# A six-product graph kernel: the first product sums x unprojected, with layer 1 behind the sum; the last half by blocks

## The chip, the cores and the metric

One core of a Trainium2 chip runs the whole kernel in one launch. The metric is the time on the device in microseconds, the median of several runs. Three runs of the kernel before took 1157.63, 1157.7 and 1158.45 us. Engines are called PE (TensorE), ACT (ScalarE), DVE (VectorE), POOL (GpSimd) and SP (SyncE, which issues most DMAs).

## What is computed

x is 4096 x 128, adj 4096 x 4096, every weight 128 x 128. Cut to what matters:

```python
def mlp(x, W1, b1, W2, b2, W3, b3):         # a = leaky_relu, slope 0.01
    return a(a(a(x @ W1 + b1) @ W2 + b2) @ W3 + b3)
u = x
for _ in range(3):
    v = mlp(adj @ u, uv_W1, uv_b1, uv_W2, uv_b2, uv_W3, uv_b3)
    u = mlp(adj @ v, vu_W1, vu_b1, vu_W2, vu_b2, vu_W3, vu_b3)   # the third u isn't needed
y = layernorm(x + v)
out = layernorm(y + adj @ (y @ gcn_W))
```

So adj is applied six times in a row (products 0 to 5), each time to something that depends on the product before.

## The kernel before

**Tiling.** A chunk is 512 nodes; there are 8. The sums are kept turned: features on the partitions, 512 nodes of the output chunk as columns, one PSUM bank each. adj is read in tiles of 128 x 1024 floats (2 x 128 input nodes times 512 output nodes). Two tiles are a band, 1 MB, one DMA. A visit multiplies one tile into one sum. Precision comes from splitting: ACT rounds a tile to `high` (L571), DVE makes `low` = raw - high (L728), and the same is done with the operand p (`p_high`, `p_low`). A visit is six products of 512 columns (L960): p_low x high and p_high x high for both halves of the tile, then p_high x low for both. Only the last two need `low`.

**Layer 1 before the sum.** Since adj @ (u @ W1) = (adj @ u) @ W1, each MLP's first layer is applied ahead of its product: `turn` multiplies a finished chunk by the next W1 and brings it back to nodes on the partitions; `raise_turned` and `lower_turned` split it into p. For product 0 this is `project_x` (PE, L893): x arrives turned, with uv_W1 in front of it (`x_turned`), is projected in FP32 chunk by chunk into PSUM banks, and ACT and DVE split it from there (`raise_x`, L575; `lower_x`, L733). x in the other order (`x_nodes`) is needed for the first layernorm's residual and is loaded into the same memory later (`load_residual`, at tile 200).

**A finished chunk.** ACT makes the first leaky layer out of the sum (`first_layer`, L623 rounded and L624 exact), DVE its low half (`lower_first`, L754), PE layer 2 in three products (`dense`, L866, L867, L869), and so on to layer 3 and the turn (`turning`, L900).

**Order of work.** `Plan` writes out by hand which visit comes when. All engines run through the same count n of visits, each in its own program order. What a chunk needs is placed at `chunk.start` plus an offset (`LOWER_FIRST`, `LAYER_2`, ... , `TURN`). ACT raises tile t `AHEAD` = 6 visits before its first visit (4 for tiles 16 to 31), DVE lowers it two visits later. SP loads bands in order; up to band 7 the loads wait for nothing, band 8 waits until DVE has lowered the tiles of band 4, band 9 for those of band 5 (a ring of four buffers). The first sweep does product 0 chunk by chunk, 16 tiles each; row c also takes the tiles of the columns 0 to c-1 a second time for product 1. `X_SPLIT` says ahead of which tile each chunk of x is split. `WARMING` FP32 products of zeros keep PE busy at first (L975).

**The tail.** The last chunk of product 5 is cut into two halves of 256 columns. Its first tiles are summed into a bank and kept in `part` (`keep`, L589). The last four tiles are visited for half 0 and then for half 1, each in a bank of its own. Per half, DVE adds bank and part (`finish_half`, L749), PE multiplies by gcn_W (`project`), DVE adds x (L787), takes statistics per block of 128 (L791, L794), ACT takes the root (L656), DVE the reciprocal (L802), and for half 1 DVE normalizes both blocks (`normalize_half`, L811).

Of the kernel before, what the change touches and what calls it, by code (L numbers as in the profile page):

```python
# [37 lines left out]
X_PIECES = [2, 2, 4]  # L38

X_SPLIT = [0, 0, 0, 0, 2, 4, 6, 8]  # L40

CONSTS_AT, OTHER_CONSTS_AT, RESIDUAL_AT = 12, 22, 200

WARMING = 9
# [11 lines left out]
FIRST = "uv_W1"  # L56
WEIGHTS = ["uv_W2", "uv_W3"]
OTHER_WEIGHTS = ["vu_W1", "vu_W2", "vu_W3", "gcn_W"]
SPLIT = ["uv_W2", "uv_W3", "vu_W2", "vu_W3"]
# [8 lines left out]

LOWER_FIRST, LAYER_2, LOWER_SECOND, LAYER_3 = 1, 3, 4, 6
# [8 lines left out]
HALF_PROJECT, HALF_MEASURE, HALF_ROOT, HALF_INVERT, HALF_NORMALIZE = 2, 3, 4, 5, 6  # L78
# [9 lines left out]
class Sum:  # L88

# [17 lines left out]
    seeded: int = -1  # L107

# [19 lines left out]
class Plan:  # L128
# [100 lines left out]
    def last_sweep(self):  # L229
# [9 lines left out]
        self.one(rows[-1], columns[:-IN_HALVES], self.open(LAST, rows[-1], "keep"))  # L239
        last = [self.tile(rows[-1], column) for column in columns[-IN_HALVES:]]  # L240
        for half in range(2):
            total = self.open(LAST, rows[-1], "finish")
            self.sums[total].half = half
            for t in last:
                self.visit(t, total)

    def place_chunks(self):
# [6 lines left out]
        for i in sorted(finished, key=lambda i: self.sums[i].closes):  # L254
            s = self.sums[i]
            if self.chunks:
                apart = SPACING[s.product] if s.product == self.sums[self.chunks[-1].total].product else BETWEEN
                s.read = max(s.read, self.chunks[-1].start + apart)
            s.finished = len(self.chunks)
            self.chunks.append(Chunk(i, s.read, s.read + (TURN if s.product < NORMED else NORM_TURN), s.half))  # L260
# [15 lines left out]
    def place_banks(self):  # L276

        holder = [None] * BANKS
        for i in sorted(range(len(self.sums)), key=lambda i: self.sums[i].opens):
            s = self.sums[i]  # L280
            s.bank = min(range(BANKS), key=lambda b: -1 if holder[b] is None else self.sums[holder[b]].read)
            if holder[s.bank] is not None:
# [19 lines left out]
def gnn_kernel(nc, adj, x_turned, x_nodes, constants, out):  # L302
# [4 lines left out]
    with ExitStack() as ctx:  # L307
# [17 lines left out]
        consts = sbuf("consts", [D, CONSTS])  # L325
        w = {name: consts[:, bass.ds(i * D, D)] for i, name in enumerate(WEIGHTS)}
        b_spread = consts[:, bass.ds(SPREAD_AT, D)]
        b = {name: consts[:, BIASES_AT + i:BIASES_AT + i + 1] for i, name in enumerate(BIASES)}
        w_high = {name: sbuf(f"w_high_{name}", [D, D], F32R) for name in SPLIT}
        w_low = {name: sbuf(f"w_low_{name}", [D, D], F32R) for name in SPLIT}  # L330

# [14 lines left out]
        sbuf("pad", [D, D])  # L346


        input_and_weight = sbuf("input", [D, D + N])
        w.update({name: consts[:, bass.ds(OTHERS_AT + i * D, D)] for i, name in enumerate(OTHER_WEIGHTS)})  # L350
        w[FIRST] = input_and_weight[:, 0:D]
        resid = input_and_weight[:, D:D + N]
# [12 lines left out]
        residual_loaded = sem("residual_loaded")  # L365
        consts_set = sem("consts_set")
        nothing_set = sem("nothing_set")
        table_loaded = sem("table_loaded")
        band_loaded = [sem(f"band_loaded{i}") for i in range(EARLY + RAWS // IN_BAND + LATE)]
# [9 lines left out]
        x_projected = sem("x_projected")  # L379
# [20 lines left out]
        normed_ready = sem("normed_ready")  # L400
        last_normed = sem("last_normed")
# [50 lines left out]
        def x_bank(c):  # L452

            return [proj, *layer, *acc[1:]][c % (BANKS + 2)]

# [11 lines left out]
        def blocks_in(i):  # L467
            half = chunks[i].half
            return range(IN_CHUNK) if half < 0 else range(half * IN_CHUNK // 2, (half + 1) * IN_CHUNK // 2)

# [43 lines left out]
        def _(sp):  # L514
            def load_x(piece):
                columns = slice(D + sum(X_PIECES[:piece]) * CHUNK if piece else 0, D + sum(X_PIECES[:piece + 1]) * CHUNK)
                sp.dma_start(input_and_weight[:, columns], x_turned[:, columns]).then_inc(x_loaded[piece], 16)

            def load_residual():
                sp.wait_ge(x_projected, CHUNKS)  # L520
                sp.dma_start(resid, x_nodes).then_inc(residual_loaded, 16)

            def load(t):
# [6 lines left out]
                sp.dma_start(band_in(buffer), adj[tiles[t][0], tiles[t][1] // IN_BAND]).then_inc(band_loaded[buffer], 16)  # L530

            for piece in range(len(X_PIECES)):
                load_x(piece)
            for t in range(0, len(tiles), IN_BAND):
                if t == CONSTS_AT:
                    sp.dma_start(consts[:, 0:OTHERS_AT], constants[:, 0:OTHERS_AT]).then_inc(consts_loaded, 16)
                if t == OTHER_CONSTS_AT:
                    sp.dma_start(consts[:, OTHERS_AT:CONSTS], constants[:, OTHERS_AT:CONSTS]).then_inc(others_loaded, 16)
                if t == RESIDUAL_AT:
                    load_residual()  # L540
                load(t)

            for i in (len(chunks) - 2, len(chunks) - 1):
                if chunks[i].half < 1:
                    sp.wait_ge(normed_ready, i - NORM + 1)
                else:
                    sp.wait_ge(last_normed, 1)
# [17 lines left out]
        def _(act):  # L565
            def split(t):
                buffer = buffers[t // IN_BAND]
                act.wait_ge(band_loaded[buffer], 16 * (len(loads_into(buffer, t // IN_BAND)) + 1))
# [4 lines left out]
            def raise_x(c):  # L573
                act.wait_ge(x_projected, c + 1)
                nc.scalar.activation(p_high[0][:, blocks_of(c)], x_bank(c)[:],  # L575
# [7 lines left out]
            def keep(s):  # L583
# [5 lines left out]
                nc.scalar.activation(part_of(s.chunk), acc[s.bank][:], ACT.Copy).then_inc(part_kept, 1)  # L589

            def seed(s):
# [5 lines left out]
                if before.goal == "keep":  # L597
                    act.wait_ge(part_kept, before.nth + 1)
                elif before.product < LAST:
# [17 lines left out]

            def first_layer(i):

                act.wait_ge(visited, sum_of(i).closes + 1)  # L620
                wait_free(i)
                bias = b[f"{way_of(i)}_b1"]
                nc.scalar.activation(h_high[:], summed(i)[:], ACT.Prelu, bias=bias, alpha=SLOPE).then_inc(first_raised, 1)  # L623
                nc.scalar.activation(h[i % 2][:], summed(i)[:], ACT.Prelu, bias=bias, alpha=SLOPE).then_inc(first_ready, 1)  # L624
# [33 lines left out]
            def normalize(i):  # L658
                act.wait_ge(shift_ready, i - NORM + 1)
                c = sum_of(i).chunk  # L660
                for j in blocks_in(i):
                    target = block_in(resid[:, blocks_of(c)] if normed(i) else part_of(c), j)
                    done = nc.scalar.activation(target, block_in(h[i % 2], j), ACT.Identity,
                                                bias=shift[:, j:j + 1], scale=rstd[:, j:j + 1])
                done.then_inc(normed_ready, 1)

# [10 lines left out]
            for n in range(END):  # L677
                if n == UV_HALVED:
                    raise_weights(SPLIT[:2])
                if n == VU_HALVED:  # L680
                    raise_weights(SPLIT[2:])
                for i, chunk in enumerate(chunks):
                    if layered(i):
                        if n == chunk.start:
# [16 lines left out]
                    if not layered(i):  # L701
                        if n == chunk.start and chunk.half < 0:
                            gather(i)
                        if n == place(i, LAST_ROOT, HALF_ROOT):
                            deviation(i)
                        if n == place(i, LAST_NORMALIZE, HALF_NORMALIZE) and chunk.half < 1:
                            normalize(i)
# [15 lines left out]
        def _(dve):  # L723
            nc.vector.memset(h[0][:, 0:D], 0.0).then_inc(nothing_set, 1)

# [5 lines left out]
            def lower_x(c):  # L731
                dve.wait_ge(p_high_ready, c + 1)
                nc.vector.tensor_tensor(p_low[0][:, blocks_of(c)], x_bank(c)[:],  # L733
# [8 lines left out]
            def finish_half(i):  # L742
# [6 lines left out]
                nc.vector.tensor_tensor(h[i % 2][:, columns], acc[s.bank][:, columns], part_of(s.chunk)[:, columns],  # L749
                                        ALU.add).then_inc(half_ready, 1)  # L750
# [18 lines left out]
            def add_bias(i):  # L769
                dve.wait_ge(proj_done, i + 1)  # L770
                nc.vector.tensor_tensor(
# [3 lines left out]
            def measure(i):  # L775

                if layered(i):
                    dve.wait_ge(leaky_done, i - NORM + 1)
                    dve.wait_ge(residual_loaded, 16)
# [6 lines left out]
                columns = columns_in(chunks[i].half)  # L786
                nc.vector.tensor_tensor(h[i % 2][:, columns], source[:, columns],  # L787
                                        resid[:, blocks_of(sum_of(i).chunk)][:, columns], ALU.add).then_inc(x_added, 1)
                dve.wait_ge(x_added, i - NORM + 1)
                for j in blocks_in(i):  # L790
                    nc.vector.bn_stats(stats[:, j, :], block_in(h[i % 2], j)).then_inc(stats_ready, 1)  # L791
# [16 lines left out]
            def normalize_half(i):  # L808

                for j in blocks_in(i):  # L810
                    done = nc.vector.tensor_scalar(block_in(part_of(sum_of(i).chunk), j), block_in(h[i % 2], j),  # L811
                                                   moments[:, j, 0:1], rstd[:, j:j + 1], op0=ALU.subtract, op1=ALU.mult)
                done.then_inc(last_normed, 1)
# [8 lines left out]
            for n in range(END):  # L822
                if n == UV_HALVED:
                    lower_weights(SPLIT[:2])
                if n == VU_HALVED:
                    lower_weights(SPLIT[2:])
                for i, chunk in enumerate(chunks):
                    if n == chunk.start and chunk.half >= 0:
                        finish_half(i)
                    if layered(i) and n == chunk.start + LOWER_FIRST:  # L830
# [15 lines left out]
                    if not layered(i):  # L846
                        if n == place(i, LAST_MEASURE, HALF_MEASURE):
                            measure(i)
                        if n == place(i, LAST_INVERT, HALF_INVERT):
                            invert(i)  # L850
                            if chunk.half == 1:
                                normalize_half(i)
# [9 lines left out]
        def _(pe):  # L862
# [7 lines left out]

            def layer_2(i):
                name = f"{way_of(i)}_W2"
                pe.wait_ge(w_low_ready, 2 if sum_of(i).product == 0 else len(SPLIT))
                if i:
                    pe.wait_ge(second_ready, i)
                else:
                    pe.wait_ge(p_low_ready, CHUNKS)
# [8 lines left out]
            def project_x(c):  # L886

                pe.wait_ge(x_loaded[0], 16)
                pe.wait_ge(x_loaded[piece_of(c)], 16)
                if c >= BANKS + 2:  # L890
# [136 lines left out]
```

## Time and profile before

| | |
|---|---|
| median of 3 runs | 1157.7 us |
| the profiled execution's own time | 1157.88 us |
| its span, first to last instruction | 1155.9 us |
| PE busy | 1149.8 us |
| DVE busy | 721.2 us |
| ACT busy | 726.6 us |
| DMA moved | 281.42 MB, mean 243 GB/s |

Busy time is summed per engine; matmuls overlap in the array, so the step from one start to the next tells more about PE than the duration of a record. A 128x128 FP32 product appears as two records. The chain is the row of work that ended last, followed back from the end: what is on it can't be shortened without the end moving, up to the point where something else is late. Idle time is given with what ended it.

### The profile page before, as it was taken

To read this page: it belongs to the slowest core of one execution; us is meant where nothing else is said; L and a number is where in the kernel's file an instruction comes from. 1 tells how busy PE (TensorE), PEld (TensorE's weight loads), DVE (VectorE), ACT (ScalarE), POOL (GpSimd) and SP (SyncE) were. 2 spreads that over 40 slices of the span, in tenths; PEclk is the share of its full clock that TensorE was granted. 3 is DMA by queue.
4 is the path that set the end of the run, shared out by engine and by line. 5 is a ranking of instruction groups with operands and counts; after the bars stand their busy time and mean duration, and the time that the engine had idled before them with its cause. 6 is when DMAs were issued, how large, how long until landed. Compare 5 with 4: busy or idle time off the path is not lost.

```text
span 1155.9 us, 14073 instructions
## 1 busy us (share of the span) xinstructions
PE 1149.8 (99%) x5314; PEld 961.3 (83%) x5314; DVE 721.2 (62%) x837; ACT 726.6 (63%) x925; POOL 4.2 (0%) x12
## 2 busy tenths in 40 slices
PE   9999999999999999999999999999999999999998
PEld 8888888888888888888888888888888888888887
DVE  6987545554665344765553585545558775459996
ACT  6876654455776444876554486544567874459884
POOL 0000000000000000000000000000000000000000
PEclk9999999999999999999999999999999999999999
DMA  9997656645855576666553584656558565579990
GB/s 384 387 365 274 231 197 244 229 178 195 319 185 207 190 276 234 242 231 255 218 182 145 196 349 182 224 197 234 198 196 327 206 230 191 216 274 371 373 382 22
DMA packets 39361, 281.42 MB, mean 243 GB/s; under 512 B 4416, under 2 KB 4800, under 8 KB 5632
## 3 DMA queue, kind: packets, MB, share of 16 engines
q1 hardware_dynamic: 38736, 278.69, 64.1%
q0 software_dynamic: 560, 1.84, 0.4%
q8 instruction: 44, 0.72, 0.2%
q14 instruction: 21, 0.17, 0.0%
HBM read 278.41 MB, written 2.10 MB: 243 GB/s over the span
## 4 chain that ended last, share of the span: by engine, by line
PE 99%; DVE 0%; issue 0%; ACT 0%; DVEq 0%
PE acc L960 90%; PE proj L900 4%; PE layer L869 1%; PE layer L866 1%; PE layer L867 1%; PE proj L975 0%; PE acc L893 0%; PE proj L893 0%; PE layer L893 0%; DVE stats L791 0%; DVE h L787 0%; DVE h L749 0%; DVE part L811 0%; ACT std L656 0%; DVEq L307 0%
## 5 line engine op out<-in xcount | busy, mean ns | idle before, releaser
L960 PE MATMUL acc<-high,p_low 128*128 128x512 f32 x1544 | 603.0, 391 | 0.0
L960 PE MATMUL acc<-high,p_high 128*128 128x512 f32 x1544 | 598.9, 388 | 0.0
L728 DVE TENSOR_TENSOR low<-raw,high 128x1024 fp32r<-128x1024 f32 x482 | 562.2, 1218 | 47.5 <-ACT high L571 46.8
L571 ACT ACTIVATE high<-raw 128x1024 fp32r<-128x1024 f32 x482 | 485.9, 1054 | 70.9 <-PE acc L960 49.0
L960 PE MATMUL acc<-low,p_high 128*128 128x512 f32 x1544 | 473.8, 388 | 0.0
L960 PEld LDWEIGHTS acc<-low,p_high 128*128 128x128 f32 x1544 | 289.1, 188 | 60.1 <-DVE low L728 0.5
L960 PEld LDWEIGHTS acc<-high,p_high 128*128 128x128 f32 x1544 | 290.1, 188 | 58.1
L960 PEld LDWEIGHTS acc<-high,p_low 128*128 128x128 f32 x1544 | 290.0, 188 | 57.8
L754 DVE TENSOR_TENSOR h_low<-h,h_high 128x512 fp32r<-128x512 f32 x40 | 27.6, 690 | 223.4 <-ACT h L624 223.4
L623 ACT ACTIVATE h_high<-acc,consts 128x512 fp32r<-128x512 f32 x40 | 27.5, 686 | 165.0 <-PE acc L960 165.0
L765 DVE TENSOR_TENSOR p_low<-proj,p_high 128x512 fp32r<-128x512 f32 x32 | 22.1, 690 | 64.1 <-ACT p_high L647 64.1
L759 DVE TENSOR_TENSOR h_low<-h,h_high 128x512 fp32r<-128x512 f32 x32 | 22.1, 692 | 54.1 <-ACT h L632 54.1
L630 ACT ACTIVATE h_high<-layer,consts 128x512 fp32r<-128x512 f32 x32 | 22.1, 689 | 41.6 <-PE layer L869 41.6
L637 ACT ACTIVATE h<-layer,consts 128x512 f32<-128x512 f32 x32 | 22.1, 690 | 40.5 <-PE layer L869 39.6
L647 ACT ACTIVATE p_high<-proj 128x512 fp32r<-128x512 f32 x32 | 19.2, 599 | 41.7 <-PE proj L900 41.7
L728 DVE TENSOR_TENSOR low<-late,high 128x1024 fp32r<-128x1024 f32 x32 | 36.9, 1216 | 0.0
L900 PEld LDWEIGHTS proj<-consts,h 128*128 128x128 f32 x256 | 33.5, 191 | 3.2 <-DVE h L749 0.8
L900 PE MATMUL proj<-consts,h 128*128 128x128 f32 x256 | 33.9, 275 | 0.6 <-DVE h L749 0.6
L632 ACT ACTIVATE h<-layer,consts 128x512 f32<-128x512 f32 x40 | 27.3, 683 | 8.9 <-PE layer L869 8.9
L571 ACT ACTIVATE high<-late 128x1024 fp32r<-128x1024 f32 x32 | 31.9, 1046 | 0.0
L589 ACT ACTIVATE part<-acc 128x512 f32<-128x512 f32 x36 | 21.4, 596 | 12.1 <-PE acc L960 10.9
L624 ACT ACTIVATE h<-acc,consts 128x512 f32<-128x512 f32 x40 | 27.3, 683 | 0.0
(60 smaller groups left out, 333.4 us busy)
## 6 DMA issues: line engine op xcount, KB each, us to landing
raw<-adj_dram SPq DMA_DIRECT2D x241, 1024.0 KB, 5.5
late<-adj_dram SPq DMA_DIRECT2D x16, 1024.0 KB, 7.4
early<-adj_dram SPq DMA_DIRECT2D x4, 1024.0 KB, 11.7
input<-x_dram SPq DMA_DIRECT2D x1, 2048.0 KB, 11.3
out_dram<-part POOLq DMA_DIRECT2D x7, 256.0 KB, 6.5
input<-x_turned_dram SPq DMA_DIRECT2D x1, 1024.0 KB, 6.9
input<-x_turned_dram SPq DMA_DIRECT2D x1, 576.0 KB, 4.1
input<-x_turned_dram SPq DMA_DIRECT2D x1, 512.0 KB, 4.9
```

The lines of the kernel that those rows point to most:

```text
L571: nc.scalar.activation(high[t % SLOTS][:], raw_of(t), ACT.Copy).then_inc(high_ready, 1)
L623: nc.scalar.activation(h_high[:], summed(i)[:], ACT.Prelu, bias=bias, alpha=SLOPE).then_inc(first_raised, 1)
L624: nc.scalar.activation(h[i % 2][:], summed(i)[:], ACT.Prelu, bias=bias, alpha=SLOPE).then_inc(first_ready, 1)
L630: nc.scalar.activation(h_high[:], layer[0][:], ACT.Prelu, bias=bias, alpha=SLOPE).then_inc(second_raised, 1)
L632: nc.scalar.activation(h[i % 2][:], layer[0][:], ACT.Prelu, bias=bias, alpha=SLOPE).then_inc(second_ready, 1)
L637: nc.scalar.activation(h[i % 2][:], layer[1][:], ACT.Prelu, bias=b[f"{way_of(i)}_b3"], alpha=SLOPE).then_inc(third_ready, 1)
L728: nc.vector.tensor_tensor(low[t % SLOTS][:], raw_of(t), high[t % SLOTS][:].bitcast(F32), ALU.subtract).then_inc(low_ready, 1)
L754: nc.vector.tensor_tensor(h_low[:], h[i % 2][:], h_high[:].bitcast(F32), ALU.subtract).then_inc(first_lowered, 1)
L759: nc.vector.tensor_tensor(h_low[:], h[i % 2][:], h_high[:].bitcast(F32), ALU.subtract).then_inc(second_lowered, 1)
L765: nc.vector.tensor_tensor(p_low[k % 2][:, blocks_of(c)], proj[:], p_high[k % 2][:, blocks_of(c)].bitcast(F32), ALU.subtract).then_inc(p_lo ...
L900: done = nc.tensor.matmul(block_in(proj, j), block_in(source, j), weight, start=True, stop=True)
L960: return nc.tensor.matmul(bank[:, into], p[parity][:, block(j)], a[slot][:, columns(j)], start=(first and n == s.opens and s.seed < 0), st ...
```

## The change

- `project_x`, `x_turned`, `load_residual` and `FIRST` go. ACT and DVE split `x_nodes` itself into p of product 0, straight from SBUF; it stays there as the residual. It is loaded in pieces of 1, 1, 2 and 4 chunks ahead of bands 0, 1, 2 and 4, and band 0 in two halves. Chunk c of x is split ahead of tile 2c.
- uv_W1 joins the split weights. When a sum of product 0 is complete, ACT rounds it (`raise_sum`), DVE makes its low half (`lower_sum`), PE multiplies by uv_W1 in three products of 512 columns (`layer_1`), and `first_layer` reads that result. The chunk's later steps begin three visits later (`FRONT`).
- Warming: 12 products of constant zeros in place of 9, with no wait for a memset.
- The bias row `b_spread` gets its own load, at tile 200.
- The tail: half 1 goes on in the bank of the kept sum, and only half 0's columns are kept. x is put into PSUM ahead of time (`seed_residuals`), and the projection adds onto it. Half 1 is copied, projected and measured by blocks of 128 columns; the last two blocks are normalized by ACT and by DVE.

```diff
-X_PIECES = [2, 2, 4]
-X_SPLIT = [0, 0, 0, 0, 2, 4, 6, 8]
-WARMING = 9
+X_PIECES = [1, 1, 2, 4]
+X_AT = [0, 2, 4, 8]
+X_SPLIT = [0, 2, 4, 6, 8, 10, 12, 14]
+WARMING = 12
+FRONT, RAISE_SUM, LOWER_SUM, LAYER_1 = 3, -3, -2, -1
-HALF_PROJECT, HALF_MEASURE, HALF_ROOT, HALF_INVERT, HALF_NORMALIZE = 2, 3, 4, 5, 6
+HALF_PROJECT, HALF_MEASURE, HALF_ROOT, HALF_INVERT, HALF_NORMALIZE = 2, 3, 4, 4, 5
...
+            self.sums[total].continues = whole if half else -1
...
+            start = s.read if s.product else s.read + FRONT
...
-                nc.scalar.activation(part_of(s.chunk), acc[s.bank][:], ACT.Copy).then_inc(part_kept, 1)
+                columns = columns_in(0 if (s.product, s.chunk) == (LAST, sum_of(len(chunks) - 1).chunk) else -1)
+                nc.scalar.activation(part_of(s.chunk)[:, columns], acc[s.bank][:, columns], ACT.Copy).then_inc(part_kept, 1)
+
+            def seed_residuals():
...
+                act.wait_ge(x_added, last - 1 - NORM)
+                nc.scalar.activation(layer[0][:, columns_in(0)], residual[:, columns_in(0)], ACT.Copy).then_inc(residual_seeded, 1)
+                for j in blocks_in(last):
+                    nc.scalar.activation(block_in(shown(last)[j], j), block_in(residual, j), ACT.Copy).then_inc(residual_seeded, 1)
...
+            def raise_sum(i):
+                act.wait_ge(visited, sum_of(i).closes + 1)
+                nc.scalar.activation(h_high[:], summed(i)[:], ACT.Copy).then_inc(sum_raised, 1)
...
+            def normalize_first(i):
+                j = blocks_in(i)[0]
+                act.wait_ge(last_centred, 1)
+                act.wait_ge(rstd_ready, i - NORM + 1)
+                nc.scalar.activation(block_in(part_of(sum_of(i).chunk), j), block_in(h[i % 2], j), ACT.Copy,
+                                     scale=rstd[:, j:j + 1]).then_inc(last_normed, 1)
...
+            def lower_sum(i):
+                dve.wait_ge(sum_raised, i + 1)
+                nc.vector.tensor_tensor(h_low[:], summed(i)[:], h_high[:].bitcast(F32), ALU.subtract).then_inc(sum_lowered, 1)
...
+            def centre(i):
+                j = blocks_in(i)[0]
+                dve.wait_ge(moments_ready, i - NORM + 1)
+                nc.vector.tensor_scalar(block_in(h[i % 2], j), block_in(shown(i)[j], j), moments[:, j, 0:1], None,
+                                        op0=ALU.subtract).then_inc(last_centred, 1)
...
+            def layer_1(i):
+                pe.wait_ge(w_low_ready, 3)
+                if i:
+                    pe.wait_ge(third_ready, i)
+                dense(layer[1], "uv_W1", i, sum_raised, sum_lowered).then_inc(layer_1_done, 1)
...
+            def project_half(i):
+                half = chunks[i].half
+                pe.wait_ge(residual_seeded, 1 + 2 * half)
+                pe.wait_ge(half_ready, half + 1)
+                for nth, j in enumerate(blocks_in(i)):
+                    if half == 1:
+                        pe.wait_ge(half_ready, half + 1 + nth)
+                    done = nc.tensor.matmul(block_in(shown(i)[j], j), block_in(h[i % 2], j), w["gcn_W"], start=False,
+                                            stop=True, skip_group_check=True)
+                    if half == 1 or nth == 1:
+                        done.then_inc(proj_done, 1)
```

## Rows read from the trace of the kernel before

**Rows 1.** The page's head and its chain by engine.
```profile
span 1155.9 us, 14073 instructions
PE 99%; DVE 0%; issue 0%; ACT 0%; DVEq 0%
```

**Rows 2.** Chain in order of time: start us, us, what.
```profile
1.05 4.21 PE proj L975 x18
12.20 0.89 PE proj L893 x8
13.10 26.11 PE acc L960 x114
39.89 4.08 PE acc L960 x18
```

**Rows 3.** Timeline, PE: start us, us, engine, line, operation, names, shape, count.
```profile
37.68 0.39 PE L960 MATMUL acc<-high,p_low 128*128 128x512 f32 x1
39.04 0.39 PE L866 MATMUL layer<-h_high,w_low_uv_W 128*128 128x512 f32 x1
```

**Rows 4.** Windows: stretch, busy of each engine, clock, DMA share, GB/s.
```profile
3.00:6.00 3.00, 3.00 (x16) 3.00 (x16) 0.00 (x0) 0.00 (x0) 0.00 (x0) 1.00 1.03 426
24.00:27.00 3.00, 3.00 (x14) 2.29 (x13) 3.00 (x4) 2.20 (x3) 0.00 (x0) 1.00 1.03 437
27.00:30.00 3.00, 3.00 (x15) 2.46 (x14) 3.00 (x4) 2.57 (x3) 0.00 (x0) 1.00 0.99 369
```

**Rows 5.** Timeline, ACT; in brackets the idle time before and its releaser.
```profile
26.77 2.01 ACT L571 ACTIVATE high<-raw 128x1024 fp32r<-128x1024 f32 x2 [0.80 <-DMA raw<-adj_dram]
29.21 2.01 ACT L571 ACTIVATE high<-raw 128x1024 fp32r<-128x1024 f32 x2 [0.43 <-DMA raw<-adj_dram]
...
35.30 2.01 ACT L571 ACTIVATE high<-raw 128x1024 fp32r<-128x1024 f32 x2 [1.56 <-DMA raw<-adj_dram]
37.21 0.67 ACT L623 ACTIVATE h_high<-acc,consts 128x512 fp32r<-128x512 f32 x1
37.78 0.68 ACT L624 ACTIVATE h<-acc,consts 128x512 f32<-128x512 f32 x1
...
41.03 1.06 ACT L571 ACTIVATE high<-raw 128x1024 fp32r<-128x1024 f32 x1 [0.67 <-DMA raw<-adj_dram]
```

**Rows 6.** Timeline, DVE, up to the second layer of chunk 0.
```profile
23.59 9.16 DVE L728 TENSOR_TENSOR low<-raw,high 128x1024 fp32r<-128x1024 f32 x8
32.68 0.48 DVE L739 TENSOR_TENSOR w_low_uv_W<-consts,w_high_uv_W 128x128 fp32r<-128x128 f32 x2
...
38.49 0.69 DVE L754 TENSOR_TENSOR h_low<-h,h_high 128x512 fp32r<-128x512 f32 x1 [0.88 <-ACT h L624]
39.10 3.49 DVE L728 TENSOR_TENSOR low<-raw,high 128x1024 fp32r<-128x1024 f32 x3
...
43.88 5.76 DVE L728 TENSOR_TENSOR low<-raw,high 128x1024 fp32r<-128x1024 f32 x5
```

**Rows 7.** DMA: the first issues; and issue, KB each, median us to landing.
```profile
0.74 1.33 SPq L517 DMA_DIRECT2D input<-x_turned_dram  x3
...
input<-x_turned_dram SPq DMA_DIRECT2D x1, 576.0 KB, 4.1
```

**Rows 8.** The turn of product 0's last chunk: PE's chain, DVE's timeline.
```profile
280.83 0.89 PE proj L900 x8
...
282.39 0.69 DVE L765 TENSOR_TENSOR p_low<-proj,p_high 128x512 fp32r<-128x512 f32 x1 [1.33 <-ACT p_high L647]
```

**Rows 9.** Chain in order of time, behind the last visit.
```profile
1150.26 0.44 DVE h L749
...
1150.74 0.73 PE proj L900 x4
...
1151.49 0.44 DVE h L787
...
1151.95 0.49 DVE stats L791 x2
1152.43 0.23 DVE moments L794 x2
...
1153.22 0.35 DVE part L811
```

More of the change, by code:

```diff
@@ L238, in last_sweep @@
         columns = self.band(rows)
-        self.one(rows[-1], columns[:-IN_HALVES], self.open(LAST, rows[-1], "keep"))
+        whole = self.open(LAST, rows[-1], "keep")
+        self.one(rows[-1], columns[:-IN_HALVES], whole)
         last = [self.tile(rows[-1], column) for column in columns[-IN_HALVES:]]
@@ L259, in place_chunks @@
             s.finished = len(self.chunks)
-            self.chunks.append(Chunk(i, s.read, s.read + (TURN if s.product < NORMED else NORM_TURN), s.half))
+            start = s.read if s.product else s.read + FRONT
+            self.chunks.append(Chunk(i, start, start + (TURN if s.product < NORMED else NORM_TURN), s.half))
     def place_parts(self):
@@ L469, in blocks_in, with shown @@
             return range(IN_CHUNK) if half < 0 else range(half * IN_CHUNK // 2, (half + 1) * IN_CHUNK // 2)
+        def shown(i):
+            if chunks[i].half < 0:
+                return [h[i % 2]] * IN_CHUNK
+            return [layer[0], layer[0], layer[1], proj]
         def measured(i):
@@ L598, in seed @@
                     act.wait_ge(part_kept, before.nth + 1)
+                elif before.product == 0:
+                    act.wait_ge(sum_lowered, before.finished + 1)
                 elif before.product < LAST:
@@ L678, in _ @@
                 if n == UV_HALVED:
-                    raise_weights(SPLIT[:2])
+                    raise_weights(SPLIT[:3])
                 if n == VU_HALVED:
-                    raise_weights(SPLIT[2:])
+                    raise_weights(SPLIT[3:])
                 for i, chunk in enumerate(chunks):
                     if layered(i):
+                        if sum_of(i).product == 0 and n == chunk.start + RAISE_SUM:
+                            raise_sum(i)
                         if n == chunk.start:
@@ L703, in _ @@
                             gather(i)
+                        if n == chunk.start - 4 and chunk.half == 0:
+                            seed_residuals()
                         if n == place(i, LAST_ROOT, HALF_ROOT):
                             deviation(i)
-                        if n == place(i, LAST_NORMALIZE, HALF_NORMALIZE) and chunk.half < 1:
-                            normalize(i)
+                        if n == place(i, LAST_NORMALIZE, HALF_NORMALIZE):
+                            if chunk.half < 1:
+                                normalize(i)
+                            else:
+                                normalize_first(i)
                 for s in sums:
@@ L778, in measure @@
                     dve.wait_ge(leaky_done, i - NORM + 1)
-                    dve.wait_ge(residual_loaded, 16)
+                    for loaded in x_loaded:
+                        dve.wait_ge(loaded, 16)
                     source = h[i % 2]
@@ L829, in _ @@
                         finish_half(i)
+                    if sum_of(i).product == 0 and n == chunk.start + LOWER_SUM:
+                        lower_sum(i)
                     if layered(i) and n == chunk.start + LOWER_FIRST:
@@ L919, in project @@
             def project(i):
[L920 to L923 removed]
+                pe.wait_ge(total_ready, i - FINAL + 1)
                 if i > FINAL:
@@ L936, in wait_bank @@
                     pe.wait_ge(part_kept, before.nth + 1)
+                elif before.product == 0:
+                    pe.wait_ge(sum_lowered, before.finished + 1)
                 elif before.product < LAST:
@@ L980, in _ @@
                     if layered(i):
+                        if sum_of(i).product == 0 and n == chunk.start + LAYER_1:
+                            layer_1(i)
                         if n == chunk.start + LAYER_2:
@@ L986, in _ @@
                             turn(i)
-                    elif n == place(i, PROJECT, HALF_PROJECT):
+                    elif chunk.half < 0 and n == chunk.start + PROJECT:
                         project(i)
+                    elif chunk.half >= 0 and n == chunk.start + HALF_PROJECT:
+                        project_half(i)
                 if n < len(visits):
```

167 lines of the change are left out of this document (88 added, 79 removed).

## The prediction, made before the change was run

> **What bounds the kernel now.** The page's head and its chain come first: TensorE is busy for 99% of the span and holds 99% of the chain [rows 1]. So the time is the work on TensorE, plus what lies before it runs without a gap, plus what lies behind its last product. The chain in order of time is read next [rows 2]. From about 1.1 us TensorE warms up, then multiplies x by uv_W1 (L893), and the sum over adjacency tiles runs from about 13 us. Six products of 512 columns make a visit; 18 of them take 4.08 us, so one product is 0.227 us and a visit 1.36 us. In PE's own rows visit 18 starts at 37.68 and the first layer product at 39.04 [rows 3]. Counting back 18 visits of 1.36 us from 37.68 gives 13.2 us: from there to the tail TensorE behaves as if it had never waited.
>
> What does the front rest on? The windows show DMA at 426 to 437 GB/s and fully busy up to 27 us [rows 4]. ACT waits for bands at 26.77 (tiles 12, 13), 29.21 (14, 15), 35.30 (18, 19) and 41.03 (22) [rows 5]. DVE lowers without a pause from 23.59 to 32.75 [rows 6]. So up to tile 22 three things are nearly level: the load, DVE, and TensorE. That decides the case: TensorE can't be brought forward by more than the data allow.
>
> **Removed from TensorE: the projection.** 32 FP32 products of 128x128 appear as 64 records. Eight take 0.89 us [rows 2], so 64 take 7.1 us (0.111 each). All of it lies before 13.2 us, partly under the wait for the first bands.
>
> **Added to TensorE: uv_W1 behind the sum.** Eight chunks of product 0, three products of 512 columns each: 24 x 0.227 = 5.44 us. It lies after 13.2 us, where TensorE has no idle time to take it in [rows 1], so it counts in full. This term is the surest.
>
> **What does the earlier start bring?** The new first load is 256 KB of x and then half a band. The old first 576 KB landed 4.1 us after an issue at 0.74 [rows 7], which is 4.85; 768 KB at 426 GB/s are 0.46 us more, 5.3. One raise takes ACT 1.06 us, so the first visit can start near 6.4, 6.8 us earlier than 13.2. The 24 warming records at 4.21 / 18 = 0.234 us take 5.6 us [rows 2], and end about there. But the amount loaded up to tile 14 stays: before 2.06 MB of x and uv_W1, eight bands, 0.14 MB of constants; after 2.00, eight, 0.20. So bands 6 and 7 land at about 26.8 and 29.2 as now. With the raise and the lowering behind them (1.06 + 1.22), and the first four products of a visit (0.91) able to run before the low half is there, tile 14 allows a start of 29.2 + 2.3 - 0.9 - 14 x 1.36 = 11.6, and tile 12 one of 11.8. The load thus caps the gain at 13.2 - 11.7 = 1.5 us, however early visit 0 runs.
>
> DVE takes most of that away. Before, four of the eight chunks of x were lowered ahead of tile 0; now chunk c waits until tile 2c. Between band 6 and band 4 lie 2.14 MB, 5.3 us, so band 4 lands near 21.4 and DVE can lower tile 8 from 22.4. From there its list up to the first new wait is: tiles 8 to 18, 11 x 1.14 us (five took 5.76, eight 9.16, less the overlap); x chunks 5, 6 and 7, 3 x 0.61 (the step from one lowering of 512 to the next operation, 38.49 to 39.10); three weights, 0.6 (two took 0.48); and lower_sum of chunk 0, 0.69 [rows 6]. The end is 22.4 + 12.5 + 1.8 + 0.6 + 0.7 = 38.0. TensorE's third layer-1 product waits for it and ends at 38.3. Before, visit 18 began at 37.68; with the 0.68 us of layer 1 added that is 38.36. The earlier start has therefore brought about nothing by there. Were the other order decisive (band 9 at 35.30, two raises, raise_sum to 37.8, then lower_sum to 38.5), it would be 0.4 us worse. The next wait: first_layer of chunk 0 stands behind tile 22 on ACT. Its band lands at 41.03 now; a raise, two leaky functions (L623, L624: a step of 0.57, the second 0.68 long) and a lowering end near 43.9. TensorE needs them at 38.3 + 4 visits + two products = 44.2. No stall, with 0.3 us of room. I take 0 for the front, between -1.5 (the load's cap) and +1.7 (one band late by a slot of 2.46 us, less this room and 0.5 for its earlier issue, since DVE finishes tile 9 sooner).
>
> TensorE's clock: the row of the granted clock reads 1.00 at every place I quote [rows 4], but 128-column records took 0.234 us each at first and 0.111 later [rows 2], thus 1.2 and then 2.4 GHz. With the new order TensorE must wait twice early, for bands 1 and 2, about 1.5 us each. *TensorE: Matmul & The Clock Gate* of the Trainium skill, section "HAM oscillation — how this bites in real kernels", says that waiting for a DMA between bursts of products can put the array back to its half clock, so that the next burst starts slow. No trace here has such a gap at full clock. By the rows alone the cost is zero until tile 8, since even at half rate the first visits fit under 22.4, where DVE's list takes over; by the page a slow stretch could reach beyond that, which is a rival below.
>
> **Waits added in rows 1 to 7 of the first sweep.** PE's layer_1 comes two visits (2.72 us) after ACT may raise the sum. A raise of 0.67, a lowering of 0.69 and, queued ahead of it on DVE, one tile's lowering of 1.22 are 2.6 us: it just fits. From there ACT and DVE gain on TensorE (0.96 and 1.14 us a tile against 1.36). All later steps of the chunk move back by three visits, nothing more. The tightest is the last chunk's turn: p of product 1 is now needed 0.89 + 3 x 1.36 = 5.0 us after it starts; the old one took from 280.83 to 283.08, 2.3 us [rows 8]. Cost 0, at most 1 us. The seeds, b_spread's load at tile 200 and the lost 2 MB reload lie beside TensorE's work: 0. uv_W1's raise and lowering are in the sum above; the other vu edits only renumber.
>
> **The tail.** Now, after the last visit, the chain is [rows 9]: add of the part 0.44, four projection records 0.73, add of x 0.44, two statistics 0.49, two aggregates, root, reciprocal, and two normalizations (0.35 in the chain, 0.60 by DVE's row). After: the part isn't added, since half 1 goes on in the bank; a 128-column copy, which I put at 0.27 between the 0.245 of one statistic and the 0.44 of a 256-column add, saves 0.17. Projection of block 0 alone, two records fewer at 0.11, saves 0.22. x is seeded in PSUM by ACT four visits ahead: the add goes, 0.46 with its step. ACT and DVE share the last two blocks: about 0.1. Sum 0.95, between 0.5 (PSUM reads slower, ACT's scale late) and 1.4 (block 1's statistic hidden as well). Half 0's new inversion stands on DVE ahead of finish_half of half 1; that cannot cost more than its two small operations, 0.3.
>
> **Sum.** 1155.9 + 5.44 + 0 - 0.95 = 1160.4 us of span. The profiled execution took 1157.88 for a span of 1155.9, 2.0 more, so 1162.4; the median of the runs was 1157.7, 0.2 below the profiled one: 1162.2, or 4.5 us slower. From the bounds: 5.44 - 1.5 - 1.4 = +2.5 gives 1160.2, and 5.44 + 1.7 - 0.5 = +6.6 gives 1164.3.
>
> **Rivals.**
> *The early start is kept.* If TensorE started at 6.4 and found every tile in time, 5.44 - 6.8 - 0.95 = -2.3: 1155.4, faster. It takes the place of my zero in the front and decides once tile 14 is raised by 6.4 + 19.0 = 25.4, so landed by 24.4. Against it: 10.7 MB at 426 GB/s are 25.1 us, and the row has 29.21 [rows 4, 5]. For it: TensorE has 12 us without useful sums. 4%.
> *No measurable change.* The load's cap is reached and the tail gives its best: 1160.2, or just inside two microseconds with a slightly better band. For it: DVE's list has no pause and any tenth per tile counts eleven times. 14%, of which 9 within 0.2%.
> *The layer-1 wait stalls in each chunk.* The fit of 2.6 in 2.72 us is tight; if a late band keeps ACT or DVE behind, seven chunks lose some 0.5 us each: 1165.7. Against it: the lead of ACT grows from row 1 on. 12%.
> *The clock falls in an early gap.* If it is down when DVE's list takes over, some 5 us at half rate (as long as the warm-up now lasts) lose 2.5 us: 1164.7. By the page on the clock gate this is what the early waits ask for; the rows give at most the gaps. 8%.
> My forecast has 62%. Measurement can tell 0.2%, 2.3 us, from no change: faster 0.04, same 0.10, slower 0.86. The range is 1159.9 to 1165.0.
>
> **What the changed profile would show.** PE's visit 0 near 6.5 with gaps until about 22; visit 18 starting near 38.3; 24 new products of 0.227 and no L893; the start of product 1 about 5.4 us later than now; no stall over 0.3 us after 45 us; behind the last visit about 2.5 us to the last normalization. Wrong: visit 18 before 37 (then the front gave more), a regular wait at layer_1, or 128-column spacing of 0.23 after 10 us.

## The result

The changed kernel takes 1163.59 us (median of 6 runs, 1162.87 to 1164.33) against 1157.88 us before (6 runs, 1157.63 to 1158.54): ratio 1.0047, 95% interval 1.0037 to 1.0057. That is 5.7 us slower; 4.5 were predicted. The profiled execution took 1163.49 us, its span is 1161.7.

First the page of the changed kernel, head and chain by engine, to be held against [rows 1]. TensorE is still busy for 99% of the span; but 3 points of its chain have gone to DVE and a DMA.

```profile
span 1161.7 us, 14047 instructions
PE 96%; DVE 2%; DMA 1%; SPq 0%; ACT 0%; issue 0%; DVEq 0%; ACTq 0%
```

The chain in order of time shows where they lie. Columns: start us, us, what.

```profile
5.80 16.60 DMA raw<-adj_dram
22.43 1.06 ACT high L593
23.52 2.36 DVE low L787 x2
25.88 0.60 DVE p_low L792
...
35.10 3.41 DVE low L787 x3
38.51 0.61 DVE h_low L817
39.16 0.50 PE layer L950
39.66 5.47 PE acc L1046 x24
...
291.51 0.89 PE proj L974 x8
```

Where the old chain was TensorE from 1.05 us on [rows 2], it now runs from a band's DMA over one raise into DVE's list, and reaches TensorE only at 39.16 us, at the last product of the new layer 1. The turn of product 0's last chunk stood at 280.83 [rows 8] and is at 291.51: 10.7 us, of which 3 x 1.36 is its later place and 6.6 the shift, the 5.44 of layer 1 and 1.14 of the front.

PE's timeline puts numbers on it (columns as in [rows 3]; in brackets the wait before it).

```profile
0.78 5.10 PE L1061 MATMUL proj<-const-float32-0.0 128*128 128x128 f32 x24 [0.78 <-PEq L1092]
6.99 0.50 PE L1046 MATMUL acc<-high,p_low 128*128 128x512 f32 x1 [1.11 <-ACT high L593]
12.47 0.50 PE L1046 MATMUL acc<-high,p_low 128*128 128x512 f32 x1 [1.95 <-ACT high L593]
23.54 0.50 PE L1046 MATMUL acc<-high,p_low 128*128 128x512 f32 x1 [1.08 <-ACT high L593]
38.24 0.39 PE L947 MATMUL layer<-h_high,w_low_first 128*128 128x512 f32 x1
38.47 0.39 PE L948 MATMUL layer<-h_high,w_high_uv_W 128*128 128x512 f32 x1
39.16 0.50 PE L950 MATMUL layer<-h_low,w_high_uv_W 128*128 128x512 f32 x1 [0.31 <-DVE h_low L817]
39.50 0.39 PE L1046 MATMUL acc<-high,p_low 128*128 128x512 f32 x1
```

Visit 0 starts at 6.99, about half a microsecond behind the forecast and 5.9 us ahead of the old kernel's, which PE's timeline of before has at 12.85. By visit 18 nothing of that is left: it starts at 39.50 against 37.68, 1.82 later, of which 0.68 is layer 1. So the front costs 1.14 us where the forecast had 0.

The tail's chain, against [rows 9]:

```profile
1156.86 0.30 DVE h L813
1157.16 0.14 issue
1157.30 0.47 PE layer L1009 x2
...
1157.86 0.49 DVE stats L862 x2
1158.36 0.23 DVE moments L865 x2
1158.59 0.03 issue
1158.61 0.35 DVE h L883
1158.96 0.15 DVE rstd L873
...
1159.20 0.40 ACT part L718
```

From DVE's first operation to the end of the span it is 1161.7 - 1156.86 = 4.84 us, before 1155.9 - 1150.26 = 5.64: 0.80 saved.

The account: 24 products x 0.227 = 5.44, front 1.14, tail -0.80, sum 5.78; the spans differ by 5.8.

### The profile page after: what moved, and what is told of

It is laid out like the page before. It is cut to its first block, busy times and chain, and to the rows that moved or that the text cites. A ratio compares the mean times of both kernels' runs of the same rounds, so it can differ in the third digit from the quotient of the medians.

```text
span 1161.7 us, 14047 instructions
## 1 busy us (share of the span) xinstructions
PE 1151.6 (99%) x5280; PEld 958.0 (82%) x5280; DVE 726.4 (63%) x844; ACT 730.7 (63%) x938; POOL 4.2 (0%) x12
## 4 chain that ended last, share of the span: by engine, by line
PE 96%; DVE 2%; DMA 1%; SPq 0%; ACT 0%; issue 0%; DVEq 0%; ACTq 0%
PE acc L1046 88%; PE proj L974 4%; PE layer L950 2%; PE layer L948 2%; PE layer L947 2%; DMA raw<-adj_dram 1%; DVE low L787 1%; SPq L533 0%; DVE p_low L792 0%; SPq L547 0%; ACT high L593 0%; DVE stats L862 0%; PE layer L1009 0%; DVE h_low L817 0%; DVE moments L865 0%
## 5 line engine op out<-in xcount | busy, mean ns | idle before, releaser
L669 ACT ACTIVATE h_high<-acc,consts 128x512 fp32r<-128x512 f32 x32 | 21.9, 686 | 123.9 <-PE acc L1046 123.9
L974 PEld LDWEIGHTS proj<-consts,h 128*128 128x128 f32 x376 | 49.1, 191 | 3.7
L974 PE MATMUL proj<-consts,h 128*128 128x128 f32 x376 | 49.4, 274 | 0.0
L817 DVE TENSOR_TENSOR h_low<-acc,h_high 128x512 fp32r<-128x512 f32 x8 | 5.5, 691 | 44.6 <-ACT h_high L657 44.6
L657 ACT ACTIVATE h_high<-acc 128x512 fp32r<-128x512 f32 x8 | 4.8, 596 | 40.0 <-PE acc L1046 40.0
```

The costliest lines, as they stand in the source:

```text
L974: done = nc.tensor.matmul(block_in(proj, j), block_in(source, j), weight, start=True, stop=True)
```

## The experiments

Each is an edit of the changed kernel, unless it says otherwise. They ran in three series; the kernel before, run beside them, had medians of 1157.84 to 1157.97 us, so the times can be held against the changed kernel's 1163.59. In an edit, ... stands for lines that aren't shown. "Visit 18" is the start of that visit, the first work of TensorE behind chunk 0's layer 1; in the changed kernel it is 39.50 us.

**1. Without layer 1.**

```diff
-FRONT, RAISE_SUM, LOWER_SUM, LAYER_1 = 3, -3, -2, -1
+FRONT = 0
...
-                        if sum_of(i).product == 0 and n == chunk.start + LAYER_1:
-                            layer_1(i)
```

> The changed kernel without its 24 layer-1 products, and without raise_sum and lower_sum; the chunk's steps start at the old places. Layer 1 of product 0 is left out of the computation, so that the time is read for the rest alone. Theory (TensorE's added work counts in full, the front is held by load and DVE): visit 17 still ends at 38.2 us, layer 2 of chunk 0 starts near 39.6 instead of 39.04 before, and the total is 1157.9 + 0.6 - 0.8 (tail) = 1157.7 us, 5.9 below the changed kernel. Rival (the removed projection of 7.1 us did free TensorE, and layer 1 only ate it up): well below before, 1151 to 1154.

Measured: 1158.29 us (11 runs, 1158.06 to 1158.79), before beside it 1157.94 (21 runs): ratio 1.0002 (0.9994 to 1.0011). Its layer 2 of chunk 0 starts at 39.53, against 39.04 [rows 3]:

```profile
39.53 0.39 PE L938 MATMUL layer<-h_high,w_low_uv_W 128*128 128x512 f32 x1
```

Its tail's first operation on DVE stands at 1150.75, 6.11 us ahead of the changed kernel's: 5.44 for the products and 0.67 for what waits at layer 1 in the front. The spans of the two profiles differ by only 5.4 (the medians by 5.3), since the last store landed later in this one. These are SP's waits, of the changed kernel and of this one:

```profile
SPq L318 <- DMA out_dram<-part: 1.3, 1, 1.3
```

```profile
SPq L318 <- DMA out_dram<-part: 2.1, 1, 2.1
```

Why that store takes 0.8 us more in this execution stays open. The kernel that has neither the projection nor the layer that replaced it is no faster than the one with the projection. Its front is 0.49 us later, and the new tail's gain is used up by that and by the store. The rival (1151 to 1154) falls. The chain shows what covered the 7.1 us of projection: TensorE waits for band 4 to be raised and lowered, and goes on from there.

```profile
22.35 1.06 ACT high L594
...
23.43 1.24 DVE low L780
...
24.71 14.98 PE acc L1035 x62
```

Band 4 is late here too, as below in the changed kernel, by about 1.1 us. A kernel without the projection and with band 4 on time wasn't run; it could be faster by about that much, not by 7.1.

**2. Layer 1 made twice.**

```diff
+                dense(layer[1], "uv_W1", i, sum_raised, sum_lowered)
                 dense(layer[1], "uv_W1", i, sum_raised, sum_lowered).then_inc(layer_1_done, 1)
```

> The changed kernel with the three layer-1 products of each of the eight chunks of product 0 made twice, with the same result. Theory (these products lie on TensorE's path in full): 24 x 0.227 = 5.44 us more, 1169.0. Rival (later waits have room that takes part of it in): 1165 to 1167.

Measured: 1169.22 us (4 runs, 1168.73 to 1169.27), 5.6 above the changed kernel; the spans differ by 1167.3 - 1161.7 = 5.6. Nothing later takes any of it in. The 0.2 beyond 5.44 lies in the front, where visit 18 without the second group would stand at 39.68 (40.38 less three products).

**3. The new tail on the kernel before.** The edit is the tail's part of the diff alone: `continues`, `seed_residuals`, `project_half`, `finish_half` by blocks, `centre`, `normalize_first`, `normalize_second`.

> The kernel before with the changed tail alone. Theory: from the end of the last visit to the end of the span 4.84 instead of 5.64 us, so 0.8 less: 1157.1 us. Rival (the tail's gain hangs on the later end or is taken back by the seeds on ACT and the inversion ahead of finish_half): 1157.9, no change.

Measured: 1156.99 us (11 runs) against 1157.94 (21 runs): ratio 0.9991 (0.9982 to 1.0). Run again in another series:

> The kernel before with the changed tail alone, again, for the comparison with the run that loads band 0 early: 1157.0 us.

1157.18 us (11 runs) against 1157.97 (20 runs), ratio 0.9994 (0.9986 to 1.0003). Both series have it 0.8 to 0.95 us below, as the chain says, though the intervals of the ratio just reach 1. It is the fastest version measured, and the only part of the change for which a gain was seen.

**4. A longer list on DVE.**

```diff
+                if c >= 5:
+                    dve.wait_ge(again, c - 5)
+                    nc.vector.tensor_tensor(h_low[:], resid[:, blocks_of(c)],
+                                            p_high[0][:, blocks_of(c)].bitcast(F32), ALU.subtract).then_inc(again, 1)
...
+                dve.wait_ge(again, 3)
```

> The changed kernel with a second, useless lowering of 512 columns on DVE beside those of x chunks 5, 6 and 7, between tiles 9 and 14. Theory (DVE's list sets visit 18): 3 x 0.61 = 1.8 us later, or somewhat more for the waits between them: visit 18 near 41.4, total 1165.5. Rival (the landing of the bands sets it): 39.5 to 39.8 and 1163.8.

Measured: 1165.38 us (4 runs, 1164.86 to 1165.55), 1.8 more. Its PE timeline has the layer waiting for DVE exactly as before, 1.71 later:

```profile
40.87 0.50 PE L956 MATMUL layer<-h_low,w_high_uv_W 128*128 128x512 f32 x1 [0.31 <-DVE h_low L823]
```

Three added operations at a step of 0.60 to 0.61 come out in full at the end of a 1165 us program.

**5. The list shortened where DVE was idle.**

```diff
-X_SPLIT = [0, 2, 4, 6, 8, 10, 12, 14]
+X_SPLIT = [0, 2, 4, 6, 8, 8, 8, 8]
```

> The changed kernel with chunks 5, 6 and 7 of x split ahead of tile 8, not of tiles 10, 12 and 14: their lowering moves into DVE's idle 1.48 us at 22. Theory (DVE's list between tile 8 and lower_sum of chunk 0 sets visit 18): the list gets 1.8 us shorter and starts 0.2 later; then ACT's raise_sum behind band 9 (37.8) is next, so visit 18 starts near 38.7 instead of 39.5, total 1162.8. Rival (the bands' landing holds the front, DVE only follows): 39.5 and 1163.6, unchanged.

Measured: 1163.04 us (5 runs, 1162.81 to 1165.0), 0.55 less, which is within the spread of the runs; the reading rests on the trace, which has visit 18 at 38.90, 0.60 earlier. DVE's own list no longer is last; ACT's raise_sum behind band 9 is, which DVE then follows. The two rows are ACT's, then DVE's timeline:

```profile
37.21 0.58 ACT L657 ACTIVATE h_high<-acc 128x512 fp32r<-128x512 f32 x1
...
37.82 0.69 DVE L817 TENSOR_TENSOR h_low<-acc,h_high 128x512 fp32r<-128x512 f32 x1
```

So 1.8 us off the list gave 0.6: the second limit lies that close behind the first. A third lies 0.3 behind that one: TensorE had work without a gap from tile 8's lowering up to layer 1 at 37.93, so it could not have reached visit 18 before 38.6, and the profile's chain runs through it:

```profile
25.06 13.00 PE acc L1046 x56
```

Its clock also fell in this execution, after a wait of 1.78 us, as the last section tells.

**6. x loaded first.**

```diff
-X_PIECES = [1, 1, 2, 4]
-X_AT = [0, 2, 4, 8]
+X_PIECES = [2, 2, 4]
+X_AT = [0, 0, 0]
```

Band 0 becomes one load again.

> The changed kernel with all of x loaded ahead of band 0 in pieces of 2, 2 and 4 chunks, and band 0 in one load. Visit 0 starts some 5 us later (near 12). Theory (band 4 landed 1.1 us late because the small early loads ran at 292 and 363 GB/s, and DVE's list starts with it): tile 8 is lowered from about 22.5 instead of 23.5, visit 18 starts near 38.7 instead of 39.5, total 1162.8. Rival (the early start of TensorE is worth something): slower, up to 1168.

Measured: 1163.88 us (5 runs, 1163.67 to 1164.14): no gain, 1.1 above what I expected. Two things were missed. DVE's list now has no pause after 12.21 us, where it lowers tile 0, so tile 8 isn't lowered before 23.71, whenever band 4 lands: the interleaved chunks of x fill the time. And TensorE lay idle for 6.1 us, and then ran at half its clock. The first windows (columns as in [rows 4]), and the first visit of PE's timeline:

```profile
9.00:12.00 3.00, 0.00 (x0) 0.00 (x0) 0.00 (x0) 0.88 (x1) 0.00 (x0) 0.55 1.01 426
12.00:15.00 3.00, 2.77 (x7) 2.19 (x8) 2.79 (x3) 3.00 (x5) 0.00 (x0) 0.50 1.02 431
...
12.23 0.79 PE L1038 MATMUL acc<-high,p_low 128*128 128x512 f32 x1 [6.10 <-ACT high L585]
12.82 0.63 PE L1038 MATMUL acc<-high,p_high 128*128 128x512 f32 x1
13.25 0.63 PE L1038 MATMUL acc<-high,p_low 128*128 128x512 f32 x1
```

The step from product to product is 0.43 us at a granted clock of 0.50 (1.2 GHz), where it is 0.227 at 1.00. After visit 0 its timeline lists no wait up to 38.68. The third layer-1 product could have followed at 39.14 and starts at 39.34, behind lower_sum. So DVE's list decides, and TensorE is only 0.2 us ahead of it: by these rows a full clock would have left visit 18 at 39.68. What the run does show is the load: band 6 is raised at 26.38, against 27.87 in the changed kernel.

**7. x first, TensorE kept at work, x split early.**

```diff
-X_SPLIT = [0, 2, 4, 6, 8, 10, 12, 14]
-WARMING = 12
+X_SPLIT = [0, 0, 0, 0, 2, 4, 6, 8]
+WARMING = 38
```

on top of experiment 6.

> The changed kernel with all of x loaded ahead of band 0, x split ahead of tiles 0, 0, 0, 0, 2, 4, 6, 8 as in the kernel before, and 38 warming products, so that TensorE is at full clock when band 0 is raised near 12.2 us. Theory (DVE's list is 1.8 us shorter than with x split to the last tile, and TensorE isn't slow as it was with x first and 12 warming products): no gap from 12.2 on, visit 17 ends near 36.8, raise_sum behind band 9 and lower_sum end near 38.0, visit 18 starts near 38.3, total 1162.5. Rival (what held the run with x first was not the clock): visit 18 at 39.3 to 39.5, 1163.7.

Measured: 1162.69 us (5 runs, 1162.52 to 1163.17), 0.9 below the changed kernel and 1.2 below experiment 6; visit 18 at 38.63, forecast 38.3. The edit changes DVE's list and the clock together (the granted clock reads 1.00 in every window up to 42 us), and no run changes one of them alone. By the trace of experiment 6 both were needed, since there the list ended at 39.30 and TensorE was ready at 39.14. Here raise_sum behind band 9 comes last again, from 36.93, as in experiment 5. Its first visit starts at 12.24, 5.2 us later than the changed kernel's, and the whole is faster: the early first visit gained nothing here.

**8. No warming.** `WARMING = 0`.

> The changed kernel without its 12 warming products. Theory (the front is set by DVE's list from tile 8 on): TensorE's first visits run at half clock, but visit 18 still starts near 39.5 us and the total stays 1163.6. Rival (TensorE itself is near the bound between 23.5 and 38 us, where it has 0.1 us of room a visit, 1.1 in all): if it is still at half clock at 23.5 it loses about 2 us, visit 18 starts near 40.5 and the total is 1164.5.

Measured: 1163.23 us (4 runs, 1163.0 to 1163.89), unchanged within the spread. The first visit runs at a step of 0.43, the second at 0.23, and the layer waits for DVE at 38.97 as it did. With the early order, warming buys nothing: the waits for bands 1, 2 and 4 are still there, only shorter for band 1 (0.64 us before 12.32).

**9. Band 0 ahead of half of x, on the kernel before with the new tail.** An attempt to use the free time at the start with the old arithmetic.

```diff
-            for piece in range(len(X_PIECES)):
-                load_x(piece)
+            load_x(0)
+            load_x(1)
             for t in range(0, len(tiles), IN_BAND):
+                if t == IN_BAND:
+                    load_x(2)
...
-            for c in range(CHUNKS):
+            for c in range(CHUNKS // 2):
                 project_x(c)
             for n in range(END):
+                if n == IN_BAND:
+                    for c in range(CHUNKS // 2, CHUNKS):
+                        project_x(c)
```

> The kernel before with the changed tail, and with band 0 loaded ahead of the last four chunks of x, whose projection comes ahead of visit 2 and no longer ahead of visit 0. Theory (before, DVE's list ran without a pause from 12.1 us; now tiles 0 and 1 are lowered ahead of that, while nothing is added to TensorE): visit 18 starts near 36.7 to 37.2 instead of 37.68 us, total 1156.99 less 0.5 to 1.0, so 1156.0 to 1156.5. Rival (band 9, behind which first_layer of chunk 0 stands on ACT, holds TensorE at its second layer at 39.0 us whatever comes earlier): no change, 1157.0.

Measured: 1158.81 us (11 runs, 1158.13 to 1159.86), 1.6 slower than the same kernel without the edit in the same series. The profiled execution took 1159.81, 1.0 above that median. In it layer 2 of chunk 0 starts at 41.91; without the edit it is 38.98 in the same series. PE's timeline, one window, and a piece of the chain:

```profile
10.35 0.50 PE L1026 MATMUL acc<-high,p_low 128*128 128x512 f32 x1 [1.63 <-ACT high L586]
...
12.56 0.63 PE L1026 MATMUL acc<-high,p_low 128*128 128x512 f32 x1
...
15.12 2.85 PE L949 MATMUL acc<-input 128*128 128x128 f32 x24
...
12.00:15.00 3.00, 3.00 (x8) 2.33 (x8) 0.69 (x1) 0.00 (x0) 0.00 (x0) 0.50 1.03 434
...
11.61 3.68 PE acc L1026 x8
```

After a wait of 1.63 us and the first products behind it the granted clock fell to 0.50, the two visits ran until 15.1, the projections behind them until 18.6, and DVE stood still for 4.16 us waiting for the x that TensorE projects there. The chain stays on TensorE from 11.61 past layer 2. Its eight products there took 3.68 us, where eight steps of 0.227 are 1.82; so up to 1.9 of the 2.9 us can be the clock. How much of that DVE's list would have taken back, and how much is the place of the projections, this run does not separate.

## Why the prediction held, and where it was off

**Layer 1, 5.44 us in full: right.** Experiments 1 and 2 take it away and double it. Taking it away moves the tail by 5.44 and the 0.67 of its wait; doubling it moves the end by 5.6.

**The projection's 7.1 us bring nothing: right.** Experiment 1 has it, within the 1.1 us by which band 4 is late there. This was the point on which the sign hung: the rival that kept the early start needed tile 14 landed by 24.4 us, and the changed kernel raises it from 30.31.

**The front, forecast 0, was 1.14.** The mechanism held: load and DVE's list keep the early start from counting. Two things in its size were wrong. The first is an input. I worked DVE's list out at 15.6 us from the first lowering of tile 8 to the end of lower_sum; it took from 23.52 to 39.12, 15.6 us. It was its start that I had 1.1 us too early: band 4 was put at 21.4 us from the old rate of 426 GB/s, and it was raised at 22.43.

The second is a choice. The prediction had two sums for the end of lower_sum, 38.0 by DVE's list and 38.5 by ACT behind band 9, and took the earlier one, though lower_sum waits for both and the later must count. Experiment 5 shows that sum by itself: raise_sum from 37.21, visit 18 at 38.90, a front of 0.54. So even with band 4 at 21.4 and band 9 as it landed, 0 was out of reach; the late band 4 added the other 0.6. The best front measured, visit 18 at 38.63 in experiment 7, is 0.27.

The windows of the changed kernel at the start:

```profile
3.00:6.00 3.00, 2.88 (x16) 2.69 (x14) 0.69 (x1) 0.75 (x2) 0.00 (x0) 1.00 0.88 292
6.00:9.00 3.00, 1.95 (x7) 1.34 (x8) 1.71 (x2) 2.10 (x3) 0.00 (x0) 1.00 1.01 363
9.00:12.00 3.00, 1.53 (x6) 0.68 (x5) 1.34 (x2) 1.16 (x2) 0.00 (x0) 1.00 1.01 404
```

Against 426 GB/s that is (134 + 63 + 22) x 3 = 657 KB short, worth 1.5 us of load, which is what band 6 gains where x comes first (27.87 to 26.38). Where x is loaded in pieces of 512 KB and more and band 0 whole (experiment 6), the windows from 3 to 12 us read 407, 421 and 426. So the small early loads of the change cost DMA rate exactly where the load is the limit. From 6 to 12 us the DMA share reads 1.01 at 363 and 404 GB/s, so there the engines were busy and moved less, and it was not work that was missing. That it is the loads' size and not their order was not separated. That the list sets the front is shown from both sides, by experiments 4 (longer, 1.8 us later) and 5 (shorter, 0.6 us earlier, then ACT behind band 9).

**The clock, a rival at 8%.** In the changed kernel's profile the granted clock reads 1.00 across the wait of 1.95 us before 12.47, and no time was lost. In experiment 2, the same program up to there, a wait of 2.24 us was followed by a fall, and the front hardly felt it (39.68 for visit 18's place, 0.18 behind the changed kernel, where band 4 was raised 0.18 later as well):

```profile
12.00:15.00 3.00, 2.31 (x6) 1.81 (x7) 2.33 (x3) 2.11 (x3) 0.00 (x0) 0.66 1.02 433
15.00:18.00 3.00, 3.00 (x11) 2.39 (x11) 2.30 (x4) 2.76 (x4) 0.00 (x0) 0.77 0.99 421
```

So the fall can happen, and tile 8's wait hides it. The prediction's count, that the first visits fit under 22.4 even at half rate, holds for the short fall seen, from 12.7 to about 16.4 us; eight visits at its step of 0.43 from 6.4 on would take until 27. The rule of the Trainium skill (*TensorE: Matmul & The Clock Gate*, "HAM oscillation — how this bites in real kernels"), that waits for a DMA between bursts put the array back to its half clock, agrees with experiments 2, 5, 6 and 9; in the profiles of the changed kernel and of experiment 4 the clock stayed up through waits of 1.95 and 1.80 us. In 2 and 5 a later wait of TensorE made the loss up, in 6 DVE's list was longer anyway, and only in 9 can it have cost time.

**The waits at layer_1 in later chunks, 12%: didn't come.** From 45 us to the tail the waits of the changed kernel show none of TensorE. The fit of 2.6 us into 2.72 held in all seven chunks.

**The tail, forecast -0.95, was -0.80.** Projection by block saved 0.26 (0.73 to 0.47; 0.22 forecast). The seeded x saved its 0.46, less 0.07, since the statistics start 0.09 us behind the projection and the add of x started 0.02 behind it. And the 128-column copy takes 0.30 and 0.14 more until TensorE starts, against 0.44 and 0.04 for the 256-column add it replaced: 0.04 saved, not 0.17. The shared normalization ends 0.40 us after its start instead of 0.60, against 0.1 forecast, and 0.05 of that is lost between the aggregates and it. Together 0.26, 0.39, 0.04 and 0.15 are 0.84; the missing 0.04 lies in the statistics (0.73 to the last aggregate's end, before 0.71) and behind the last operation. Half 0's inversion ends at 1156.81, just before finish_half starts at 1156.86. The last visit's last product starts at 1156.37 as a record of 0.40 for two; before, DVE also started 0.09 behind its end, so the inversion cost nothing, though with no room.

**The sum.** The span was forecast at 1160.4 and came out at 1161.7. The front's 1.14 and the tail's 0.15 make up the difference; both went the same way, so the forecast was not right by errors of the two that cancelled. Inside the tail some did: the copy and the seed gave 0.20 less than forecast, projection and normalization 0.09 more.

## What to carry to other kernels

Before work is moved from in front of the main loop to inside it, ask which engine is waiting in front of it: here TensorE's 7.1 us of projection lay under the load and its splitting on ACT and DVE, and 5.44 us went to a stretch without a gap. An earlier first instruction is worth only what the last of the level resources allows; count the ordered list of the second engine from the load that starts it to the first thing the busy engine needs. Where two such sums bound the same operation, take the later. And when loads are cut up to let the first tile in early, read the DMA rate of those first microseconds again.

## What the runs showed of the hardware that was not expected

After 6.10 us without work TensorE's first products stepped by 0.43 us, and the granted clock read 0.50 (experiment 6); after 1.63 us it fell too (experiment 9). The changed kernel and experiments 2, 4 and 5 have the same program up to tile 8, the same warming products and visits 0 and 1, and then a wait for band 1. After waits of 1.95 us (changed kernel) and 1.80 (experiment 4) the clock stayed at 1.00; after 2.24 (experiment 2) it read 0.66 from 12 to 15 us, and after 1.78 (experiment 5) 0.64:

```profile
12.00:15.00 3.00, 2.50 (x7) 1.92 (x8) 2.52 (x3) 1.92 (x3) 0.00 (x0) 0.64 1.02 431
```

So the length of the gap alone does not decide; nearly equal gaps gave either clock from one execution to the next. The clock's mean over the whole span was 0.998 in the profiles of experiments 2 and 5 and 1.0 in the changed kernel's, but 0.998 in three of its other five executions. A fall in those too is likely, and not shown.

One repeat of the kernel with the new tail had a span of 1156.1 us where its twin had 1155.1, and its profile shows one wait for DVE more, in the second layer of chunk 1:

```profile
65.75 0.50 PE L923 MATMUL layer<-h_low,w_high_uv_W 128*128 128x512 f32 x1 [0.48 <-DVE h_low L798]
```

Its chain, from 39 to 65 us, passes twice through the load of a band, where its twin's stays on TensorE:

```profile
40.59 7.62 DMA raw<-adj_dram
...
54.88 7.86 DMA raw<-adj_dram
```

So in this pair the difference of 1 us is made between 39 and 70 us, where load, DVE and TensorE are nearly level. After that the two profiles keep their distance to the end.
